# Scatter-add in two column halves, first rows loaded by SyncE, pad list without gaps, late weights in parts

## The reference

```
# layer 0: modulated linear, one vector y per batch
x = x + ((x * ys) @ weight) * d          # ys = y / sqrt(512), d = rsqrt((ys*ys) @ (weight*weight) + 1e-8)
# layer 1: one shared expert and the top 2 of 8 routed ones
shared = silu(xf @ w1) * (xf @ w3) @ w2                       # hidden size 1024
s = sigmoid(concat([xf, cond]) @ router_W);  top 2 of s + router_bias
gates = s_sel / (s_sel.sum + 1e-9)                            # 1/2 each if the sum is tiny
routed = sum over the 2 experts of gate * (gelu(xf @ W1e[e]) @ W2e[e])   # hidden size 512
x = x + (shared + routed) / 3
```

## Time and profile before

| | |
|---|---|
| median of 3 runs | 1156.8 us (1154.67 to 1170.54) |
| profiled execution | 1156.24 us, span 1154.4 us, granted clock 0.977 |
| PE busy | 1075.8 us (93%), 4976 instructions |
| DVE / ACT / POOL busy | 479.2 / 315.3 / 232.6 us |
| chain that ended last | PE 54%, DMA 32%; by line DMA out<-ys,slot 15%, DMA xs_d<-xrow,sadr 11% |
| scatter-add L1112 | 71 instructions, mean 1559 ns on POOL |

### The profile page before, as it was taken

How to read it: one execution, slowest core, us unless ns; L and a number is a source line. 1 busy time by engine, 2 the same in 40 slices (tenths; PEclk the granted TensorE clock), 3 DMA queues, 4 the chain that set the end, 5 groups by cost and what they waited for, 6 DMA issues and landing times.

```text
span 1154.4 us, 15574 instructions
## 1 busy us (share of the span) xinstructions
PE 1075.8 (93%) x4976; PEld 875.0 (76%) x4977; DVE 479.2 (42%) x759; ACT 315.3 (27%) x488; POOL 232.6 (20%) x253
## 2 busy tenths in 40 slices
PE   7999899999999999999964989999998799999996
PEld 6778787888888888888843868777787587777874
DVE  5554556685333333333201134444443244444442
ACT  4332432323222222222101123333332133333331
POOL 0000000001113343433451001122311122322222
PEclk9999999999999999999986999999998899999999
DMA  4566578778765777776537059854588855546453
GB/s 166 192 201 232 209 247 274 274 256 246 241 235 185 259 258 235 258 253 232 151 128 148 0 184 275 230 104 82 82 235 254 252 122 100 82 82 101 81 83 45
DMA packets 119773, 209.86 MB, mean 182 GB/s; under 512 B 23920, under 2 KB 78320, under 8 KB 108464
## 3 DMA queue, kind: packets, MB, share of 16 engines
q1 hardware_dynamic: 55136, 142.22, 36.8%
q0 software_dynamic: 25440, 48.38, 19.9%
q10 hardware_dynamic: 39168, 18.88, 6.9%
HBM read 111.01 MB, written 98.65 MB: 182 GB/s over the span
## 4 chain that ended last, share of the span: by engine, by line
PE 54%; DMA 32%; issue 5%; DVE 3%; POOL 2%; SPq 2%; ACT 1%; ACTq 0%; POOLq 0%; DVEq 0%
DMA out<-ys,slot 15%; DMA xs_d<-xrow,sadr 11%; PE banks L486 7%; PE banks L488 7%; PE banks L487 7%; PE banks L422 6%; PE banks L423 6%; PE banks L424 5%; PE banks L436 3%; PE banks L437 3%; PE banks L438 3%; DMA we_d<-ehl 2%; PE banks L388 2%; PE banks L390 2%; PE banks L389 2%
## 5 line engine op out<-in xcount | busy, mean ns | idle before, releaser
L422 PE MATMUL banks<-xh,w13h 128*128 128x512 f32 x512 | 199.5, 390 | 1.9 <-DVE w13l L735 1.9
L423 PE MATMUL banks<-xl,w13h 128*128 128x512 f32 x512 | 199.2, 389 | 0.0
L424 PE MATMUL banks<-xh,w13l 128*128 128x512 f32 x512 | 199.2, 389 | 0.0
L1112 POOL DMA_INDIRECT out<-ys,slot x71 | 110.7, 1559 | 425.5 <-DMA out<-ys,slot 273.8
L757 DVE SCALAR_TENSOR_TENSOR gm<-sil,banks 128x512 f32<-128x512 f32 x64 | 43.9, 686 | 270.1 <-ACT sil L579 270.0
L486 PE MATMUL banks<-we,hidth 128*128 x284 | 115.9, 408 | 16.1 <-issue 13.7
L436 PE MATMUL banks<-wmh,gh 128*128 128x512 f32 x256 | 100.9, 394 | 31.2 <-DVE outst L769 29.0
L486 PE MATMUL banks<-we,xgth 128*128 x284 | 118.6, 418 | 7.2 <-issue 6.6
L579 ACT ACTIVATE sil<-banks 128x512 f32<-128x512 f32 x64 | 38.1, 595 | 316.8 <-PE banks L424 273.5
L488 PE MATMUL banks<-we,hidtl 128*128 x284 | 113.4, 399 | 0.0
L487 PE MATMUL banks<-we,hidth 128*128 x284 | 113.1, 398 | 0.0
(11 more groups left out here) (155 smaller groups left out, 1490.9 us busy)
## 6 DMA issues: line engine op xcount, KB each, us to landing
we_d<-ehl SPq DMA_DIRECT2D x32, 1024.0 KB, 6.3
we<-we_d SPq DMA_DIRECT2D x16, 2048.0 KB, 9.2
xg<-xs_d ACTq DMA_DIRECT2D x144, 128.0 KB
eraw<-expert_w SPq DMA_DIRECT2D x32, 512.0 KB, 5.8
xin<-xT SPq DMA_DIRECT2D x8, 1024.0 KB, 6.5
x1t_d<-x1t SPq DMA_DIRECT2D x8, 1024.0 KB, 8.5
xin<-x1t_d SPq DMA_DIRECT2D x8, 1024.0 KB, 9.1
x_d<-x1tok SPq DMA_DIRECT2D x32, 256.0 KB
```

The lines of the kernel that those rows point to most:

```text
L422: pe.matmul(ps[hc % 2][:, :], w_hi, xh[:, j, c, :], start=(c == 0), stop=False)
L423: pe.matmul(ps[hc % 2][:, :], w_hi, xl[:, j, c, :], start=False, stop=False)
L424: last = pe.matmul(ps[hc % 2][:, :], w_lo, xh[:, j, c, :], start=False, stop=(c == DC - 1))
L1112: pool.indirect_dma_start(out[:, :], IO(slot[:, t, 0:1], 0), ys[:, t % RING, :], None, compute_op=ALU.add).then_inc(added, 16)
```

## The change

- `scatter` becomes two accumulating DMAs per tile, columns 0 to 255 and 256 to 511, onto a view of `out` with rows of 256. Each half has its own semaphore, `added[0]` and `added[1]`, and waits only for the same half of the tile before. DVE works out the doubled indices `row2` once, in two instructions, and `take_y` waits for both halves.
- The rows of the first four tiles are loaded by SP, after its own wait for the scatters, instead of by ACT ahead of block 7; the wait of ACT goes too.
- `pad_rows` makes a list of exactly the unused slots: 9,216 - 8,192 = 1,024, so 8 scatters of 128 (`PADS`) instead of 16. DVE takes some more small instructions for it.
- The weights of turns 4 to 7 are loaded in parts of 512 KB, each awaited before the next, instead of in halves of 2 MB.

```
         @block.sync   (after weight_loaded(0))
-            sp.wait_ge(pad_out, 16 * 2 * E)
+            sp.wait_ge(xl_ready, DC * 2 * NBLK)
+            sp.wait_ge(x1_turned, DC * NBLK)
+            sp.wait_ge(pad_out, 16 * PADS)
             for b in range(XB):
                 sp.wait_ge(xrow_out[b], 16 * (K * NT // XB))
+            for j in range(RING // PAIR):
+                for g in range(P // Q):
+                    sp.dma_start(xg[g * Q:(g + 1) * Q, j * PAIR:(j + 1) * PAIR].rearrange("p t a n -> p (t a) n"),
+                                 xs_d[j * PAIR * P:(j + 1) * PAIR * P, g * P:(g + 1) * P].rearrange("(a r) d -> r a d", r=Q)).then_inc(xg_in[j], 16)
             sp.dma_start(slot[:, :, :], xs_rec).then_inc(slots_in, 16)
...
+            def load_in_parts(i, e, place):
+                for q in range(4):
+                    sp.dma_start(we[:, bass.ds(place, 1), i % 2, q // 2, q % 2].rearrange("p a c n -> p (a c n)").bitcast(FP32),
+                                 we_d[bass.ds(e * 4 + i % 2 * 2 + q // 2, 1), :, q % 2].rearrange("a p n -> p (a n)").bitcast(FP32)).then_inc(we_in[i % HRING], 16)
+                    sp.wait_ge(we_in[i % HRING], 16 + 16 * (q + 1))
+                sp.sem_inc(weights_in, 1)
...
                 for i in (2 * r, 2 * r + 1):
-                    load_weight(i, e, bass.ds(place, 1))
-                    weight_loaded(i)
+                    load_in_parts(i, e, place)
         @block.scalar   (ahead of block_steps(NBLK - 1, 1, None, False))
-            act.wait_ge(xl_ready, DC * 2 * NBLK)
-            act.wait_ge(pad_out, 16 * 2 * E)
-            for b in range(XB):
-                act.wait_ge(xrow_out[b], 16 * (K * NT // XB))
-            load_rows(0, 0, 0)
-            load_rows(PAIR, PAIR, 0)
         @block.vector
                 if reused:
-                    dve.wait_ge(added, 16 * (t + 1 - RING))
+                    for h in range(2):
+                        dve.wait_ge(added[h], 16 * (t + 1 - RING))
...
             dve.wait_ge(slots_in, 16)
+            for h in range(2):
+                dve.tensor_scalar(row2[:, h, :], slot[:, :, 0], 2.0, float(h), ALU.mult, ALU.add).then_inc(halved, 1)
         @block.gpsimd
-            for g in range(2 * E):
+            for g in range(PADS):
...
+            out_half = out.rearrange("t (h d) -> (t h) d", h=2)
             def scatter(t):
                 pool.wait_ge(ys_done, t + 1 + 2)
-                if t:
-                    pool.wait_ge(added, 16 * t)
-                pool.indirect_dma_start(out[:, :], IO(slot[:, t, 0:1], 0), ys[:, t % RING, :], None,
-                                        compute_op=ALU.add).then_inc(added, 16)
+                for h in range(2):
+                    if t:
+                        pool.wait_ge(added[h], 16 * t)
+                    pool.indirect_dma_start(out_half, IO(row2[:, h, t:t + 1], 0), ys[:, t % RING, h * D // 2:(h + 1) * D // 2], None,
+                                            compute_op=ALU.add).then_inc(added[h], 16)
```

More of the change, by code:

```diff
@@ L36 @@
 Q = 32
+PADS = (SLOTS - K * TOK) // P
 ROW = D + 2
@@ L105, in shared_moe_kernel @@
         xgt = sb("xgt", [2, DC, P], FP32, 192)
+        row2 = sb("row2", [2, PADDED], INT32, 196)
         x1tok = sb("x1tok", [BLK // Q, DC, Q], FP32, 168)
@@ L145, in shared_moe_kernel @@
         sadr = small("sadr", [K, NT], INT32)
-        padr = small("padr", [2 * E], INT32)
+        padr = small("padr", [PADS], INT32)
         pad = small("pad", [3, 2 * E])
@@ L167, in shared_moe_kernel @@
         x1_d = nc.dram_tensor("x1_d", [TOK, D], FP32)
-        xs_d = nc.dram_tensor("xs_d", [SLOTS + P, ROW], FP32)
+        xs_d = nc.dram_tensor("xs_d", [SLOTS, ROW], FP32)
         we_d = nc.dram_tensor("we_d", [EP, P, 2, PIECE], FP32R)
@@ L213, in shared_moe_kernel @@
         ys_done = sem("ys_done")
-        added = sem("added")
+        halved = sem("halved")
+        added = [sem(f"added{h}") for h in range(2)]
         block = ctx.enter_context(nc.Block())
@@ L350, in _ @@
                 for i in (2 * r, 2 * r + 1):
-                    load_weight(i, e, bass.ds(place, 1))
-                    weight_loaded(i)
+                    load_in_parts(i, e, place)
             sp.wait_ge(pads_in, 16)
             sp.wait_ge(out_stored, 16 * NBLK)
-            sp.wait_ge(added, 16 * TILES)
+            for h in range(2):
+                sp.wait_ge(added[h], 16 * TILES)
         @block.tensor
@@ L869, in pad_rows @@
             def pad_rows():
[L871 to L882, removed]
@@ L883, in pad_rows @@
-                then(dve.tensor_tensor(begin, begin, upto, ALU.mult))
-                then(dve.tensor_scalar(begin, begin, dummy[:, 0:1], None, ALU.add))
-                dve.tensor_copy(padr[:, :], begin).then_inc(pad_done, 1)
+                begin, free, sums = (pad[:, r, :] for r in range(3))
+                count = row(PING)[:, NT - 1, :]
+                place = row(PONG)[:, 0, 0:PADS]
+                grid = row(PONG).rearrange("p a b -> p (a b)")[:, E:E + PADS * (E + 1)].rearrange("p (g e) -> p g e", e=E + 1)
@@ new lines, in pad_rows @@
+                then(dve.tensor_tensor(begin[:, 0:E], e8[:, 4, :], count, ALU.add))
+                then(dve.tensor_scalar(begin[:, E:E + 1], e8[:, 1, E - 1:E], float(P), None, ALU.mult))
+                then(dve.scalar_tensor_tensor(free[:, 1:E + 1], e8[:, 0, :], float(P), count, ALU.mult, ALU.subtract))
+                then(dve.tensor_scalar(free[:, 0:1], begin[:, 0:1], 0.0, None, ALU.mult))
+                src, dst = free, sums
+                for d in (1, 2, 4, 8):
+                    dve.tensor_copy(dst[:, 0:d], src[:, 0:d])
+                    then(dve.tensor_tensor(dst[:, d:E + 1], src[:, d:E + 1], src[:, 0:E + 1 - d], ALU.add))
+                    src, dst = dst, src
@@ new lines, in pad_rows @@
+                then(dve.tensor_tensor(begin[:, 0:E + 1], begin[:, 0:E + 1], src[:, 0:E + 1], ALU.subtract))
+                then(dve.tensor_copy(place, tid[:, 0:PADS]))
+                then(dve.tensor_tensor(grid, place.unsqueeze(2).to_broadcast([P, PADS, E + 1]),
+                                       src[:, 0:E + 1].unsqueeze(1).to_broadcast([P, PADS, E + 1]), ALU.is_ge))
+                then(dve.tensor_tensor(grid, grid, begin[:, 0:E + 1].unsqueeze(1).to_broadcast([P, PADS, E + 1]), ALU.mult))
@@ L887, in slot_rows @@
+                then(dve.tensor_reduce(dst[:, 0:PADS], grid, AX.X, ALU.max))
+                then(dve.tensor_tensor(dst[:, 0:PADS], dst[:, 0:PADS], place, ALU.add))
+                dve.tensor_copy(padr[:, :], dst[:, 0:PADS]).then_inc(pad_done, 1)
             def slot_rows():
@@ L1094, in _ @@
                 pool.indirect_dma_start(xs_d[:, :], IO(padr[:, g:g + 1], 0), xrow[:, XB - 1, :], None).then_inc(pad_out, 16)
-            pool.wait_ge(pad_out, 16 * 2 * E)
+            pool.wait_ge(pad_out, 16 * PADS)
             load_row(XB - 1)
@@ L1104, in _ @@
                         load_row(m + XB)
-            pool.wait_ge(slots_in, 16)
+            pool.wait_ge(halved, 2)
+            out_half = out.rearrange("t (h d) -> (t h) d", h=2)
             def scatter(t):
                 pool.wait_ge(ys_done, t + 1 + 2)
-                if t:
-                    pool.wait_ge(added, 16 * t)
-                pool.indirect_dma_start(out[:, :], IO(slot[:, t, 0:1], 0), ys[:, t % RING, :], None,
-                                        compute_op=ALU.add).then_inc(added, 16)
+                for h in range(2):
+                    if t:
+                        pool.wait_ge(added[h], 16 * t)
+                    pool.indirect_dma_start(out_half, IO(row2[:, h, t:t + 1], 0), ys[:, t % RING, h * D // 2:(h + 1) * D // 2], None,
+                                            compute_op=ALU.add).then_inc(added[h], 16)
             pool.wait_ge(out_stored, 16 * NBLK)
```

## The result

The changed kernel takes 1101.3 us (median of 4, 1100.8 to 1101.64) against 1163.7 for the kernel before in the same comparison (1154.67 to 1171.8): a ratio of 0.9465, interval 0.9376 to 0.9555. The profiled execution takes 1101.17 us; its span is 1099.4 us and its mean clock 0.993. On another chip the two stood at 1100.7 and 1155.8, ratio 0.952 (0.9475 to 0.9566). The direction was forecast; the size was not: 1113 was said, with 1104 as the low end, and 11 us are missing.

A forecast was written before the change was run, and what follows sets the result against it. PE's own work was taken as the bound, with gains only in two dips: 1156.2 - 30.0 (part 1) - 15.6 (parts 3 and 4) + 1.5 + 0.4 = 1112.5 us, said as 1113, range 1104 to 1132.

The forecast's parts named there:

- part 4: Stage 3 scatters as two chains: 5.1 us per tile, no gain outside weight loads; closes part 3's 3 us, 1.5 left.
- Quiet tiles: Stage 3 outside the dips: PE needs 6.2 us per tile, so two chains gain nothing there.
- The first loads: Weight loads of turns 0 to 3, still 2 MB: cost PE about 1.9 us near 748 us, left as is.
- The late loads: Second dip, 845 to 927 us, loads for turns 4 to 7: costs PE 17.1 us, of which 15.6 is won.
- The end: Last tile: second half issued 1.9 us after the first, lands up to 0.7 sooner than a whole; +1.5 us.
- part 1: Block 7, first rows loaded by SP: PE's 28.05 us stall and its low clock go, 30.0 us together.
- Part 2: Eight pad scatters: POOL starts placing 39 us sooner, placements end at 600 to 613 us; costed at nothing.
- The longer pad list: DVE in block 1: 7 to 9 more small instructions, under 2 us, costing PE nothing.
- Part 3: Late weights in 32 awaited 512 KB parts, 200 us instead of 83; alone leaves about 3 us of stall.
- Contention by pieces: Rival: scatters lose fixed time per descriptor beside weight loads, so halves lose twice, 12.3 us per tile; 1128 us, chance 0.14.
- The slower case: Rival: scatter chain bounds all stage 3, up to 7.6 us per tile, 1210 us; chance 0.06.

The follow-up runs named there:

- whole_row: Changed kernel with one accumulating DMA of 512 columns per tile again, all else as changed; 1112.3 us.
- whole_parts: Changed kernel with one DMA of 512 columns per tile again and the weight loads of turns 1 to 3 in 512 KB parts too; 1108.1 us.
- best: Changed kernel with the old list of 16 pads and the weight loads of turns 1 to 3 in parts too; 1099.7 us, ratio 0.9502.
- rows_only: Kernel before with only the first four tiles' row loads moved to SP and ACT's wait for the placements gone; 1132.5 us, ratio 0.979.
- one_chain: Changed kernel with the two halves in one chain, each half waiting for the one before to land; 1318.0 us, one run.
- quarters: Changed kernel with four scatter chains of 128 columns instead of two of 256; 1212.3 us, one run.
- hoist: best with PE's expert number and place loaded once per tile, ahead of the previous tile's transposes, except each four's first; 1101.1 us.

## Why the prediction was wrong

**The step that failed** is the worth of the two chains in part 4: "Outside the weight loads this gains nothing, PE needs 6.2 us." It took PE's pace of 6.2 us as PE's own and the chain's 5.6 as safely faster. What the runs showed in its place: with whole rows put back (whole_row) the kernel takes 1112.3 us, so the halves bring 11 us, as much as was missing, where the forecast gave them next to nothing, and the largest term lies outside the weight loads. Two things are behind it. The first is the lag: at 5.6 against 6.1 us a lag of 20 us takes some 40 tiles to work off, so a load episode can meet a ring that is half full. Halves do 4.71 us per tile while catching up ((762.04 - 714.98)/10; I had taken 5.1), and the lag is gone at tile 17. The second is not the lag, since whole_parts has none and is still 8.4 us slower than best from the first to the last gelu. The terms of the sum:

- *Quiet tiles*: 0.1 us per tile that I called PE's own pace, 5.2 us here. whole_parts shows that most of it goes with whole rows as such, at the head of a tile, where PE's register loads take longer beside them (whole_parts against best).
- *The first loads*, left as they were in the forecast: the step behind gelu 10 was 8.26 us and is 5.94. 2.5 us in this profile; in the second profile of the changed kernel a step of 6.92 remained there.
- *The late loads*: 17.1 us by the windows and 1.5 left as stall; by the gelus 18.7 us were to be had, and all went. 3.1 us. The stall that was left came from the 33 us that the parts were to cost the chain. They cost a chain of whole rows 14 us, and it had no stall beside them with a lag of 11 to 12 us in the ring (whole_row).
- *The end*: forecast 1.5 us longer, in fact 1.3 shorter. 2.8 us. From the last `ys` to the last landing it is 0.9 us longer, as forecast in kind: the second half is issued 1.9 us after the first and lands in 3.8 us instead of 4.6. But from this landing to the end of the span it takes 1.5 us instead of 3.8, for which the forecast had no term.

```profile
1146.05 1.56 POOL L1112 DMA_INDIRECT out<-ys,slot  x1 [3.75 <-DVE ys L1025]
...
out<-ys,slot POOLq DMA_INDIRECT x1, 4.6
```

```profile
out<-ys,row POOLq DMA_INDIRECT x1, 3.8
```

(The kernel before, then the changed one, whose last issue is shown above.) In every profile in which the last landing shows, seven with whole rows and six with halves, the rest is 3.8 and 1.5 us; in both it is POOL's closing instruction that ends late. Why it ends sooner behind halves stays open. The four terms are 13.6 us; stage 3 began 2.3 us later than forecast, which leaves 11.3.

**Right as reckoned**: part 1. The stall is gone (the gelus and the gates of block 7 come 30.2 us sooner against those of block 6; forecast 30.0), nothing took its place, and rows_only shows that it needs none of the other parts. Part 2: the placing began at 317.5 instead of 364.1, and its last scatter, 608.67, is 1.8 us sooner than before, for the reason given. The longer pad list was costed at nothing and costs 0.6 us: from block 2's third step on the gates are that much later in all nine profiles with the new list, and in none of those with the old one. Block 6 was 2.6 us later than before; the other 2.0 us lie in stage 1, which the change does not touch; there the profiles lie 1.8 us before to 3.0 us behind that of the kernel before. Part 3: 32 loads of 512 KB, 4.4 us to landing, from 813 to 977 us, 164 us instead of the 200 reckoned, and no stall beside them.

**The rivals.** Contention by pieces did not bring its time: under the first loads a tile took (714.98 - 668.57)/5 = 9.3 us, not 12.3, and 10.2 before. But its mechanism is real, and I was wrong to expect the loss to go by bytes. In one_chain, where the halves do not wait at the same time, a half beside loads of 2 MB loses 5.1 us, as much as a whole row with its 5.3, and a tile takes 19.0 us. Beside the parts its tile loses 1.4 us (9.9 against 8.5), that of whole_row 0.5. What saved the changed kernel is the point that the prediction put against this rival: its two halves wait at the same time. The time that the DMA engines work does go by bytes: a tile's two halves hold each engine for 42.7% of 80 us over 16 tiles, 2.1 us, against 2.0 for the whole row. The rule of the Trainium skill cited there ("DMA: Bandwidth & Descriptors", section "Queues, rings and completion order"), turns by whole packets, would let the loss grow with the number of turns; one_chain agrees with that, 19.0 us for two halves against 10.2 for one whole. The slower case, the chain as the bound, did not come with two chains, but it is real: one_chain and quarters are it, with 8.4 to 9.9 and 7.5 us per tile.

What stays open: why PE's register loads take longer beside whole rows, why the end is shorter behind halves, and why runs of the kernel before differ by up to 19 us on one chip, where those of the changed kernel differ by 1 to 5; the lag at the end is a candidate, but no profile of a long run was taken.

## What to carry to other kernels

A serial chain that is 10% faster than its producer is not off the path: after each disturbance compute how long it takes to catch up, how much room the ring has when the next one starts, and what lag is left at the end; a deeper ring only moves the lag to the end. Splitting a chained transfer pays while its latency, and not its bytes or the issuing engine's instruction, is the larger part, and only if the parts run as chains of their own; beside bulk loads each part waits as long as the whole did (one_chain). A wait that an in-order queue executes before work that does not need it is the cheapest thing to move.

## What was not expected of the hardware

- An accumulating indirect DMA of 128 rows holds POOL 1.56 us at 512, 256 and 128 columns alike, and lands in 4.7 us at 512 and 3.6 to 3.8 at 256.
- A chain of whole rows ran at 9.2 to 10.2 us per tile beside 2 MB loads and, with a lag to work off, at 6.2 beside awaited 512 KB parts, while these moved their 2 MB in some 20 us (4 x 4.4 and the turns) instead of 9.
- With run-time values on PE a tile's pace depended on what the DMA engines scattered (6.18 against 6.08 us); with constants it was 5.935 us in both. A register load on PE's queue took 0.30 us undisturbed, up to 0.8 beside halves (hoist) and up to 1.26 beside whole rows (whole_parts).
- Beside 2 MB loads a half in one chain landed in 7.6 to 10.3 us, a whole row in 8.0 to 10.6.
- The span ends 3.8 us after the last landing with whole rows and 1.5 us after it with halves.
